# Applying the error's rows in half passes: key tiles 0 and 1 of a test-time-memory attention kernel

## The chip, the cores and the metric

One Trainium2 chip, one core. The metric is device time in microseconds (us) of one launch, lower is better.

## What is computed

Two layers over 8 sequences of 512 tokens with 128 features, all in fp32. Each layer is `x = x + s * g`, with `s` from a sequence mixer and `g` a SiLU of a feed-forward part. The change lies in the second layer's mixer, a memory that is trained while it reads. Per head (8 of them) and chunk of 64 tokens, the gradient of a two-matrix MLP's loss is taken, run through momentum and decay, added to the weights, and read with the queries:

```python
grads = jax.vmap(jax.grad(chunk_loss), ...)(mem_ws, flat(keys), lr, flat(values))
surprise = -grads
momentum = _assoc_scan(gm, surprise)
updates = _assoc_scan(gd, momentum)
w0 = mem_w0 + updates[0]
w1 = mem_w1 + updates[1]
x = jnp.einsum('bhncd,bhnde->bhnce', q, w0)
vals = jnp.einsum('bhncd,bhnde->bhnce', jax.nn.silu(x), w1)
```

The feed-forward part of that layer sends each token to one of 8 experts.

## The kernel before

The kernel never forms the updated weights. The update of a weight matrix is a weighted sum over earlier tokens of key times error, so reading it with a query is a score (key by query) times a coefficient, applied to the error's rows. This is linear attention with per-chunk coefficients, once for each of the two matrices.

After the first layer, `attend` runs 64 heads (8 batches by 8 heads). Its `step(f, s, z)` is written once for each engine, and every engine runs its own instructions strictly in that order. One step holds the front of head n + 1 (f), the second half of head n (s) and the end of head n - 1 (z). In batches 2 to 6 (`X_FIRST` to `X_LAST`) a step also carries one block x of 128 tokens of an expert's feed-forward: 40 steps in all. I call them expert heads, the others plain heads.

In a step TensorE (`pe`) does the following.
- It projects head f to U, EB and QA, and computes the second scores of head s, `scores(..., p_s1)`. In an expert head it transposes the block's rows (L813).
- It computes the product with s_2 into EB (the prediction's error) and the product of xs_2 into VB. To VB it adds `apply(VB, err_t, v_p1, k)`, with four key tiles i of 450, 322, 194 and 66 query columns.
- It does the expert block's first product (L828, expert heads), transposes err (L834) and multiplies err back through w1 into U (err_high, w4t).
- It computes the first scores of head f, transposes du, projects with w_x, and runs `apply(XB, du_t, v_p0, n)`. Then come the expert block's second product, the output product (L864) and the sums of squares (L868).

A product is either plain fp32, which the profile shows as two records, or `product(...)`: both operands are split into a high and a low fp32r half, and three passes high*high, high*low, low*high are added. The split costs a copy to fp32r (ScalarE) and a subtract (VectorE or GpSimd, called POOL in the profile). Before the change, both applies are plain fp32.

The scores get their coefficients on VectorE (`dve`): `weigh` multiplies the four tiles in the order 0, 1, 3, 2 (`SC_ORDER`) into p_sb and counts v_p1 (or v_p0) up after tiles 0, 3 and 2:

```python
                        if i != 1:
                            last.then_inc(done, 1)
```

In an expert head weigh comes after xf, the block's scaled input, which waits for the transpose L813. After weigh VectorE makes q_sb (L1109, L1111; the first of these counts v_q, and TensorE may overwrite U only after it), err_low (L1115), and du (L1118) after TensorE's product.

ScalarE (`act`) copies results out of PSUM and makes high halves: xs, s, th, qa, err, vals, sq, err_t, hid (expert heads), du_t, sq_mid. In heads 1 to 8 `scale_rows` (four rows) and in batch 7 `gate_rows` (four rows of a finished batch) stand ahead of du_t.

POOL makes the low halves of s, qa and sq, the root rs (which waits for VectorE's ms) and rg, which VectorE's sum of the outputs waits for before it weighs. In heads 6 to 13 it also issues four scatters each, in heads 5 to 10 it makes `starts`. In batch 7 it multiplies a finished batch by its gate (L1251), and VectorE adds the residual (L1164) before the next ms.

## Time and profile before

| | |
|---|---|
| median of 3 runs | 1116.36 us |
| the runs | 1113.86, 1116.40, 1116.36 us |
| the profiled execution's own time | 1116.89 us |
| its span on the core (first to last instruction) | 1115.1 us |
| mean granted TensorE clock | 0.988 of full speed |

The profile is of one execution. PE is TensorE's matmuls and PEld its weight loads, DVE is VectorE, ACT ScalarE, POOL GpSimd. Matmuls overlap in a pipeline and their ends are modelled, so two that follow each other closely show durations that add up to more than the time they take together. A row gives a group's first start, its length, the engine, the line of the kernel, the operation with output and inputs by name, the shapes and the count. Behind some stands the idle time before it and what ended that.

### The profile page before, as it was taken

Reading aid. Unit: us, or ns where it says so; the run is one execution under the profiler, and the core shown is the slowest. Engines: PE = TensorE matmul, PEld = TensorE weight load, DVE = VectorE, ACT = ScalarE, POOL = GpSimd, SP = SyncE. Lnnn points to the kernel's source line nnn. Section 1 sums busy time; section 2 is a strip of 40 time slices with the busy share of each in tenths; the row PEclk is TensorE's granted clock in tenths of the full one; section 3 lists DMA queues with packets and bytes.
Section 4 is the critical chain, followed back from the end, with each engine's and each line's share of the span. In section 5 each row is a group of like instructions: output and inputs, shape, how many; then the busy total and the mean of one; then the engine's idle time right before and its main releaser. Section 6 shows DMA issues by size and latency. Waiting matters only on the chain. (4 is left out here: it accounts for less than half of the span.)

```text
span 1115.1 us, 19052 instructions
## 1 busy us (share of the span) xinstructions
PE 1073.0 (96%) x6613; PEld 900.3 (81%) x6613; DVE 678.8 (61%) x1752; ACT 677.0 (61%) x1356; POOL 561.4 (50%) x574
## 2 busy tenths in 40 slices
PE   6999799999999999999999999999999999999994
PEld 4666588888888888888888888888888888888783
DVE  5887566766765555565555555565556555566664
ACT  5776366666655656565556655565656555566663
POOL 6885244478874444344534444344434454444453
PEclk9999699999999999999999999999999999999998
DMA  7210300000030000000000000000000000011221
GB/s 204 81 44 29 104 1 1 1 15 30 20 96 14 19 10 9 8 21 10 9 11 9 19 11 8 9 20 11 8 8 11 20 10 6 3 53 49 69 69 42
DMA packets 42129, 32.66 MB, mean 29 GB/s; under 512 B 4042, under 2 KB 36652, under 8 KB 41900
## 3 DMA queue, kind: packets, MB, share of 16 engines
q1 hardware_dynamic: 38484, 25.93, 8.1%
q0 software_dynamic: 2304, 4.74, 1.3%
q8 instruction: 54, 0.88, 0.3%
q10 hardware_dynamic: 1248, 0.79, 0.2%
q14 instruction: 39, 0.32, 0.1%
HBM read 18.30 MB, written 13.41 MB: 28 GB/s over the span
## 5 line engine op out<-in xcount | busy, mean ns | idle before, releaser
L1040 DVE TENSOR_TENSOR p_sb<-bank,coef 128x512 f32<-128x512 f32 (+3 forms) x512 | 218.7, 483 | 3.1 <-PE bank L749 2.6
L1232 POOL TENSOR_TENSOR sq_rest<-sq,sq_high 128x450 f32<-128x450 f32 x64 | 67.0, 1048 | 243.7 <-ACT sq_high L934 243.7
L772 PE MATMUL bank<-p_sb,du_t 128*128 128x450 f32 (+3 forms) x512 | 130.1, 397 | 4.4 <-ACT du_t L950 4.4
L772 PE MATMUL bank<-p_sb,err_t 128*128 128x450 f32 (+3 forms) x512 | 132.9, 402 | 0.2 <-DVE p_sb L1040 0.2
L772 PEld LDWEIGHTS bank<-p_sb,du_t 128*128 128x128 f32 x512 | 82.1, 190 | 48.9 <-issue 23.9
L772 PEld LDWEIGHTS bank<-p_sb,err_t 128*128 128x128 f32 x512 | 83.7, 190 | 45.6 <-DVE p_sb L1040 25.2
L1236 POOL TENSOR_TENSOR sq_low<-sq_rest,sq_mid 128x450 bf16<-128x450 f32 x64 | 67.5, 1054 | 104.3 <-ACT sq_mid L953 104.1
L1093 DVE SCALAR_TENSOR_TENSOR acc<-bank,rg,acc 128x128 f32<-128x128 f32 x224 | 62.8, 343 | 68.0 <-POOL rg L1220 68.0
L903 ACT ACTIVATE xs<-bank 128x450 f32<-128x450 f32 x64 | 35.0, 547 | 107.4 <-PE bank L772 107.4
L1118 DVE SCALAR_TENSOR_TENSOR du<-q_sb,bank 128x512 f32<-128x512 f32 x64 | 44.1, 689 | 89.0 <-PE bank L749 89.0
L1216 POOL TENSOR_TENSOR rs<-ms,neg_half 128x4 f32<-128x4 f32 x64 | 80.5, 1258 | 28.2 <-DVE ms L1075 26.8
L1207 POOL TENSOR_TENSOR s_low<-s_sb,s_high 128x512 fp32r<-128x512 f32 x64 | 82.6, 1291 | 21.6 <-ACT s_high L911 21.4
L909 ACT ACTIVATE s_sb<-bank 128x512 f32<-128x512 f32 x64 | 38.3, 598 | 88.5 <-PE bank L749 88.4
L930 ACT COPY vals<-bank 128x450 f32<-128x450 f32 x64 | 34.3, 536 | 88.8 <-PE bank L772 88.8
L1246 POOL DMA_INDIRECT ffn_rows<-xl_all,ids x40 | 41.5, 1038 | 83.9 <-DVE xl_all L1126 83.9
L1126 DVE TENSOR_TENSOR xl_all<-bank,xl_all 128x128 f32<-128x128 f32 x40 | 11.7, 292 | 117.2 <-PE bank L858 117.2
L1207 POOL TENSOR_TENSOR qa_low<-qa,qa_high 128x450 fp32r<-128x450 f32 x64 | 74.4, 1163 | 13.6 <-ACT qa_high L921 13.3
L924 ACT COPY err<-bank 128x512 f32<-128x512 f32 x64 | 37.6, 587 | 60.1 <-PE bank L749 60.1
L864 PE MATMUL bank<-w_out,vals 128*128 128x128 f32 (+1 forms) x512 | 67.4, 274 | 0.6 <-ACT vals L930 0.6
L864 PEld LDWEIGHTS bank<-w_out,vals 128*128 128x128 f32 (+1 forms) x512 | 60.0, 179 | 0.9 <-ACT vals L930 0.9
L950 ACT COPY du_t<-bank 128x512 f32<-128x512 f32 x64 | 37.3, 582 | 26.7 <-PE bank L848 26.7
L764 PE MATMUL bank<-qa,yb 128*128 128x66 f32 (+1 forms) x256 | 52.9, 288 | 0.0
(297 smaller groups left out, 3094.5 us busy)
## 6 DMA issues: line engine op xcount, KB each, us to landing
sorted_rows<-coef SPq DMA_DIRECT2D x5, 516.0 KB, 5.0
rows<-sorted_rows SPq DMA_DIRECT2D x40, 64.5 KB, 1.8
x<-in_L_attn_inputs SPq DMA_DIRECT2D x8, 256.0 KB, 5.5
x_rows<-x SPq DMA_DIRECT2D x8, 256.0 KB, 2.3
ew<-in_L_ffn_w SPq DMA_DIRECT2D x8, 256.0 KB, 4.0
attn_out<-acc SPq DMA_DIRECT2D x7, 256.0 KB, 2.1
ew<-attn_out SPq DMA_DIRECT2D x7, 256.0 KB
ew<-ffn_rows SPq DMA_DIRECT2D x8, 192.0 KB
```

The lines of the kernel that those rows point to most:

```text
L764: last = pe.matmul(out, left[:, (i - 2) * P:(i - 1) * P], right[:, P * i:], start=True, stop=True)
L772: last = pe.matmul(out[:, P * i:QW], rows[:, i, :], p_sb[:, P_COL[i]:P_COL[i] + QW - P * i], start=False, stop=True, skip_group_check=True)
L864: pe.matmul(VB[0:r, t * P:t * P + P], vals[:, t * P:t * P + r], m.w_out[:, s[1], :], start=True, stop=True)
L909: nc.scalar.activation(s_sb[h % 2][:], U[:], ACT.Silu).then_inc(a_s, 1)
L1040: last = nc.vector.tensor_tensor(dst, src, w, ALU.mult)
L1093: last = nc.vector.scalar_tensor_tensor(sums, o, g, sums, ALU.mult, ALU.add)
L1118: nc.vector.scalar_tensor_tensor(du[:], q_sb[:], 0.5, U[:], ALU.mult, ALU.mult).then_inc(v_du, 1)
L1207: nc.gpsimd.tensor_tensor(parts[1][:], whole[:], parts[0][:], ALU.subtract).then_inc(done, 1)
L1216: nc.gpsimd.tensor_tensor(rs[:], ms[:], m.neg_half[:, 0:T], ALU.pow).then_inc(g_rs, 1)
L1232: nc.gpsimd.tensor_tensor(sq_rest[:], sq[:], sq_3[0][:], ALU.subtract).then_inc(g_rest, 1)
L1236: nc.gpsimd.tensor_tensor(sq_3[2][:], sq_rest[:], sq_3[1][:], ALU.subtract).then_inc(g_lo, 1)
L1246: nc.gpsimd.indirect_dma_start(m.ffn_rows, bass.IndirectOffsetOnAxis(ids[r][:, 0:1], axis=0), y[r], None).then_inc(s_y[r], 16)
```

## The change

Only the apply of the error's rows changes its arithmetic; that of du stays plain fp32. Key tiles 0 and 1 of it become three passes of halves each. The rows err_t of tiles 0 and 1 are split in high and low (err_t2), as are the weighed scores of these tiles (p_2). Tiles 2 and 3 stay plain fp32 and are now applied first, in the order 3, 2, then 0, 1.

For that ScalarE gets two copies p_high behind qa_high, makes err_t in two copies of 256 columns (the first to th, which is free by then), and makes errt_high behind du_t. VectorE gets two subtracts p_low behind weigh, and q_sb moves behind err_low. POOL gets the subtract errt_low behind its last scatter, ahead of starts and of the next head's rs. ScalarE's scaled and gated rows are now done two by two, the first pair ahead of vals, the second behind sq_mid (`rows_of`). To make room in SBUF, du uses err's tile, sq_rest sq's, and token_q and per_token lie in m.amd. The semaphores' counts follow.

```diff
-        err_t = sb("err_t", [P, T, D])
-        du = sb("du", [P, S])
+        err_t, err_t2 = sb("err_t", [P, 2, D]), pair("errt2", [P, 2, D])
+        du = err
         du_t = sb("du_t", [P, T, D])
-        p_sb = sb("p_sb", [P, P_COLS])
+        p_sb, p_2 = sb("p_sb", [P, P_COLS]), pair("p2", [P, 2 * QW - P])
...
-        sq_rest = sb("sq_rest", [P, QW])
...
-        token_q = sb("token_q", [P, 3, NT])
+        token_q = m.amd[:, :, E + 3:].rearrange("p n a -> p a n")[:, 0:3, :]
...
-                def apply(out, rows, made, n):
-                    for i in SC_ORDER:
+                def apply_plain(out, rows, made, n, tiles=SC_ORDER):
+                    for i in tiles:
                         if i != 3:
                             pe.wait_ge(made, SC_BANKS * n + {0: 1, 1: 2, 2: 3}[i])
                         last = pe.matmul(out[:, P * i:QW], rows[:, i, :], p_sb[:, P_COL[i]:P_COL[i] + QW - P * i],
                                          start=False, stop=True, skip_group_check=True)
+                    return last
+
+                def apply(out, plain, halves, made, n, high, low):
+
+                    pe.wait_ge(made, SC_BANKS * n + 3)
+                    for i in (3, 2):
+                        pe.matmul(out[:, P * i:QW], plain[:, i - 2, :], p_sb[:, P_COL[i]:P_COL[i] + QW - P * i],
+                                  start=False, stop=True, skip_group_check=True)
+                    for i in (0, 1):
+                        cols = QW - P * i
+                        p_high, p_low = (part[:, QW * i:QW * i + cols] for part in p_2)
+                        pe.wait_ge(high, 2 * n + i + 1)
+                        for rows in halves:
+                            pe.matmul(out[:, P * i:QW], rows[:, i, :], p_high, start=False, stop=True, skip_group_check=True)
+                        pe.wait_ge(low, 2 * n + i + 1)
+                        last = pe.matmul(out[:, P * i:QW], halves[0][:, i, :], p_low, start=False, stop=True, skip_group_check=True)
                     return last
...
-                        pe.wait_ge(a_et, k + 1)
+                        pe.wait_ge(g_el, k + 1)
                         product(VB[:, 0:QW], [w[:] for w in w1], [part[:] for part in xs_2])
-                        apply(VB, err_t, v_p1, k).then_inc(p_v, 1)
+                        apply(VB, err_t, err_t2, v_p1, k, a_p1, v_l1).then_inc(p_v, 1)
...
-                        pe.wait_ge(a_et, n + 1)
+                        pe.wait_ge(a_et, 2 * n + 1)
                         project(XB, m.w_x, f, SHIFT)
                         pe.wait_ge(a_dt, n + 1)
-                        apply(XB, du_t, v_p0, n).then_inc(p_x, 1)
+                        apply_plain(XB, du_t, v_p0, n).then_inc(p_x, 1)
...
+                def p_high_of(made, n, i, done):
+
+                    cols = QW - P * i
+                    act.wait_ge(made, SC_BANKS * n + i + 1)
+                    nc.scalar.copy(p_2[0][:, QW * i:QW * i + cols], p_sb[:, P_COL[i]:P_COL[i] + cols]).then_inc(done, 1)
...
+                def rows_of(s, tiles):
+
+                    k, c = n_of(s), last_head(s)
+                    if c is not None and c > 0:
+                        gate_rows(c - 1, tiles)
+                    if 1 <= k <= B:
+                        scale_rows(k - 1, tiles)
...
+                        act.wait_ge(g_el, n)
...
+                        p_high_of(v_p1, k, 0, a_p1)
+                        p_high_of(v_p1, k, 1, a_p1)
+                    if f is not None:
                         act.wait_ge(p_e, n + 1)
                         act.wait_ge(p_d, n)
                         nc.scalar.copy(err[:], EB[:]).then_inc(a_err, 1)
                         act.wait_ge(a_err, n + 1)
                         nc.scalar.copy(err_2[0][:], err[:]).then_inc(a_eh, 1)
+                        rows_of(s, (0, 1))
...
-                    if f is not None:
-                        act.wait_ge(p_et, n + 1)
-                        nc.scalar.copy(err_t[:].rearrange("p t d -> p (t d)"), XB[:]).then_inc(a_et, 1)
                     if x is not None:
                         act.wait_ge(p_h, x + 1)
                         for k4 in range(FB):
                             last = nc.scalar.activation(hid[:, k4, :], QA[:, k4 * P:k4 * P + P], ACT.Relu, bias=w1s[:, PAR + 2 + k4:PAR + 3 + k4])
                         last.then_inc(a_h, 1)
-                    c = last_head(s)
-                    if c is not None and c > 0:
-                        gate_rows(c - 1)
-                    if s is not None and 1 <= k <= B:
-                        scale_rows(k - 1)
                     if f is not None:
+                        act.wait_ge(p_et, n + 1)
+                        act.wait_ge(v_g, n + 1)
+                        nc.scalar.copy(th[:, 0:2 * D], XB[:, 0:2 * D])
+                        nc.scalar.copy(err_t[:].rearrange("p t d -> p (t d)"), XB[:, 2 * D:]).then_inc(a_et, 1)
                         act.wait_ge(p_dt, n + 1)
                         nc.scalar.copy(du_t[:].rearrange("p t d -> p (t d)"), EB[:]).then_inc(a_dt, 1)
+                        act.wait_ge(a_et, 2 * n + 1)
+                        nc.scalar.copy(err_t2[0][:].rearrange("p t d -> p (t d)"), th[:, 0:2 * D]).then_inc(a_et, 1)
                     if s is not None:
                         act.wait_ge(g_rest, k + 1)
-                        nc.scalar.copy(sq_3[1][:], sq_rest[:]).then_inc(a_mid, 1)
+                        nc.scalar.copy(sq_3[1][:], sq[:]).then_inc(a_mid, 1)
+                    if s is not None:
+                        rows_of(s, (2, 3))
...
+                def p_low_of(made, n, i, done):
+
+                    cols = QW - P * i
+                    p = p_sb[:, P_COL[i]:P_COL[i] + cols]
+                    dve.wait_ge(made, 2 * n + i + 1)
+                    high, low = (part[:, QW * i:QW * i + cols] for part in p_2)
+                    nc.vector.tensor_tensor(low, p, high, ALU.subtract).then_inc(done, 1)
...
+                        p_low_of(a_p1, k, 0, v_l1)
+                        p_low_of(a_p1, k, 1, v_l1)
                     if f is not None:
+                        dve.wait_ge(a_eh, n + 1)
+                        nc.vector.tensor_tensor(err_2[1][:], err[:], err_2[0][:], ALU.subtract).then_inc(v_el, 1)
...
-                        dve.wait_ge(a_eh, n + 1)
-                        nc.vector.tensor_tensor(err_2[1][:], err[:], err_2[0][:], ALU.subtract).then_inc(v_el, 1)
...
+                        pool.wait_ge(a_et, 2 * n + 2)
+                        flat = [part[:].rearrange("p t d -> p (t d)") for part in err_t2]
+                        nc.gpsimd.tensor_tensor(flat[1], th[:, 0:2 * D], flat[0], ALU.subtract).then_inc(g_el, 1)
```

On TensorE, in an expert head, from the product of xs_2 to the block's first product. Before, with the semaphores that each row waits for:

```order
L749 MATMUL bank<-xs_high,w1n_high 128x450 [waits a_et,v_acc]
L749 MATMUL bank<-xs_low,w1n_high 128x450
L749 MATMUL bank<-xs_high,w1n_low 128x450
L772 MATMUL bank<-p_sb,err_t 128x450 [waits v_p1]
L772 MATMUL bank<-p_sb,err_t 128x322 [waits v_p1]
L772 MATMUL bank<-p_sb,err_t 128x66
L772 MATMUL bank<-p_sb,err_t 128x194 [waits v_p1]
L828 MATMUL bank<-xl_all 128x128 [waits a_qa,v_xf]
```

and now:

```order
L749 MATMUL bank<-xs_high,w1n_high 128x450 [waits g_el,v_acc]
L749 MATMUL bank<-xs_low,w1n_high 128x450
L749 MATMUL bank<-xs_high,w1n_low 128x450
L780 MATMUL bank<-p_sb,err_t 128x66 [waits v_p1]
L780 MATMUL bank<-p_sb,err_t 128x194
L787 MATMUL bank<-p_high,errt_high 128x450 [waits a_p1]
L787 MATMUL bank<-p_high,errt_low 128x450
L789 MATMUL bank<-p_low,errt_high 128x450 [waits v_l1]
L787 MATMUL bank<-p_high,errt_high 128x322 [waits a_p1]
L787 MATMUL bank<-p_high,errt_low 128x322
L789 MATMUL bank<-p_low,errt_high 128x322 [waits v_l1]
L844 MATMUL bank<-xl_all 128x128 [waits a_qa,v_xf]
```

The wait for v_p1 was one per tile (tile 0's first) and is now one for all, ahead of tile 3; tiles 0 and 1 are six passes with waits for ScalarE (a_p1) and VectorE (v_l1).

On VectorE, in an expert head, from the block's scaled input (L1102, now L1147) on. Before:

```order
L1102 TENSOR_SCALAR xl_all<-bank,xl_all 128x128 [waits p_t,v_w]
L1040 TENSOR_TENSOR p_sb<-bank,coef 128x512 [waits p_s1,p_x]
L1040 TENSOR_TENSOR p_sb<-bank,coef 128x384 [waits p_s1]
L1040 TENSOR_TENSOR p_sb<-bank,coef 128x128
L1040 TENSOR_TENSOR p_sb<-bank,coef 128x256 [waits p_s1]
L1109 SCALAR_TENSOR_TENSOR q_sb<-bank,s_sb 128x512 [waits a_s,a_tu]
L1111 SCALAR_TENSOR_TENSOR q_sb<-thu,q_sb 128x512 [waits v_q]
L1115 TENSOR_TENSOR err_low<-err,err_high 128x512 [waits a_eh]
```

and now:

```order
L1147 TENSOR_SCALAR xl_all<-bank,xl_all 128x128 [waits p_t,v_w]
L1077 TENSOR_TENSOR p_sb<-bank,coef 128x512 [waits p_s1,p_x]
L1077 TENSOR_TENSOR p_sb<-bank,coef 128x384 [waits p_s1]
L1077 TENSOR_TENSOR p_sb<-bank,coef 128x128
L1077 TENSOR_TENSOR p_sb<-bank,coef 128x256 [waits p_s1]
L1087 TENSOR_TENSOR p_low<-p_sb,p_high 128x450 [waits a_p1]
L1087 TENSOR_TENSOR p_low<-p_sb,p_high 128x322 [waits a_p1]
L1155 TENSOR_TENSOR err_low<-err,err_high 128x512 [waits a_eh]
L1158 SCALAR_TENSOR_TENSOR q_sb<-bank,s_sb 128x512 [waits a_s,a_tu]
L1160 SCALAR_TENSOR_TENSOR q_sb<-thu,q_sb 128x512 [waits v_q]
```

Two subtracts are added, and err_low now stands ahead of both steps of q_sb.

On ScalarE, in an expert head, from the high half of qa on. Before:

```order
L921 CAST qa_high<-qa 128x450 [waits a_qa]
L924 COPY err<-bank 128x512 [waits p_d,p_e]
L926 CAST err_high<-err 128x512 [waits a_err]
L930 COPY vals<-bank 128x450 [waits p_o,p_v]
L932 ACTIVATE sq<-vals 128x450 [waits a_v]
L934 CAST sq_high<-sq 128x450 [waits a_sq]
L937 COPY err_t<-bank 128x512 [waits p_et]
L941 ACTIVATE xl_all<-bank,xl_all 128x128 [waits p_hh]
```

and now:

```order
L952 CAST qa_high<-qa 128x450 [waits a_qa]
L899 CAST p_high<-p_sb 128x450 [waits v_p1]
L899 CAST p_high<-p_sb 128x322 [waits v_p1]
L959 COPY err<-bank 128x512 [waits p_d,p_e]
L961 CAST err_high<-err 128x512 [waits a_err]
L966 COPY vals<-bank 128x450 [waits p_o,p_v]
L968 ACTIVATE sq<-vals 128x450 [waits a_v]
L970 CAST sq_high<-sq 128x450 [waits a_sq]
L974 ACTIVATE xl_all<-bank,xl_all 128x128 [waits p_hh]
L974 ACTIVATE xl_all<-bank,xl_all 128x128 x3
L979 COPY thu<-bank 128x256 [waits v_g,p_et]
L980 COPY err_t<-bank 128x256
```

Two copies stand ahead of err; the copy err_t is halved and moved behind the block's hidden layer (L941, now L974), and errt_high stands ahead of sq_mid.

## Rows read from the trace of the kernel before

**Rows 1.** The page's part 1: busy time of each engine, share of the span, instructions

```profile
PE 1073.0 (96%) x6613; PEld 900.3 (81%) x6613; DVE 678.8 (61%) x1752; ACT 677.0 (61%) x1356; POOL 561.4 (50%) x574
```

**Rows 2.** Windows view, batch 7: length, busy us (count) PE, PEld, DVE, ACT, POOL, clock, DMA

```profile
1010.00:1090.00 80.00, 77.12 (x468) 64.65 (x468) 52.52 (x133) 53.37 (x106) 39.34 (x38) 1.00 0.20 61
```

**Rows 3.** Timeline, TensorE, an expert head: start us, length us, engine, line, operation

```profile
712.33 0.31 PE L749 MATMUL bank<-xs_high,s_high 128*128 128x322 f32 x1
712.48 0.31 PE L749 MATMUL bank<-xs_low,s_high 128*128 128x322 f32 x1
...
714.14 0.37 PE L749 MATMUL bank<-xs_high,w1n_high 128*128 128x450 f32 x1
714.35 0.37 PE L749 MATMUL bank<-xs_low,w1n_high 128*128 128x450 f32 x1
...
714.77 2.12 PE L772 MATMUL bank<-p_sb,err_t 128*128 128x450 f32 x8
716.73 1.05 PE L828 MATMUL bank<-xl_all 128*128 128x128 f32 x8
...
717.97 0.48 PE L749 MATMUL bank<-err_high,w4t_high 128*128 128x512 f32 x1
```

**Rows 4.** Timeline, TensorE, a plain head: apply, its tiles 3 and 2, what follows

```profile
300.44 2.01 PE L772 MATMUL bank<-p_sb,err_t 128*128 128x450 f32 x8
...
301.74 0.55 PE L772 MATMUL bank<-p_sb,err_t 128*128 128x66 f32 x3
...
302.29 0.27 PE L834 MATMUL bank<-ident,err 128*128 128x128 f32 x1
...
302.64 0.48 PE L749 MATMUL bank<-err_high,w4t_high 128*128 128x512 f32 x1
```

**Rows 5.** Timeline, VectorE's weigh in that expert head; TensorE and VectorE, the last one

```profile
714.04 1.68 DVE L1040 TENSOR_TENSOR p_sb<-bank,coef 128x512 f32<-128x512 f32 x4
...
982.82 0.65 PE L772 MATMUL bank<-p_sb,err_t 128*128 128x450 f32 x1
...
983.34 0.42 DVE L1040 TENSOR_TENSOR p_sb<-bank,coef 128x256 f32<-128x256 f32 x1
```

**Rows 6.** Timeline, ScalarE, the expert head

```profile
714.34 0.59 ACT L924 COPY err<-bank 128x512 f32<-128x512 f32 x1 [0.95 <-PE bank L749]
714.96 0.62 ACT L926 CAST err_high<-err 128x512 fp32r<-128x512 f32 x1
```

**Rows 7.** Timeline, VectorE and ScalarE, the plain head (the first is tile 2's weighing)

```profile
300.07 0.41 DVE L1040 TENSOR_TENSOR p_sb<-bank,coef 128x256 f32<-128x256 f32 x1
...
300.40 0.68 DVE L1109 SCALAR_TENSOR_TENSOR q_sb<-bank,s_sb 128x512 f32<-128x512 f32 x1
301.11 0.85 DVE L1111 SCALAR_TENSOR_TENSOR q_sb<-thu,q_sb 128x512 f32<-128x512 f32 x1
...
300.65 0.62 ACT L926 CAST err_high<-err 128x512 fp32r<-128x512 f32 x1
```

**Rows 8.** The page's part 5, applies of du; timeline, a head of batch 7

```profile
L772 PE MATMUL bank<-p_sb,du_t 128*128 128x450 f32 (+3 forms) x512 | 130.1, 397 | 4.4 <-ACT du_t L950 4.4
...
1045.47 1.65 ACT L883 ACTIVATE ew<-ew,token_q 128x128 f32<-128x128 f32 x4
...
1046.69 0.37 PE L749 MATMUL bank<-y_high,w_x_low 128*128 128x450 f32 x1
1047.64 0.65 PE L772 MATMUL bank<-p_sb,du_t 128*128 128x450 f32 x1 [0.57 <-ACT du_t L950]
```

**Rows 9.** Timeline, POOL in head 8, and TensorE's product that follows

```profile
253.52 0.79 POOL L1203 TENSOR_TENSOR ew<-lr_gate,starts 128x256 f32<-128x256 f32 x1
254.27 1.44 POOL L1216 TENSOR_TENSOR rs<-ms,neg_half 128x4 f32<-128x4 f32 x1
...
256.04 1.29 POOL L1207 TENSOR_TENSOR s_low<-s_sb,s_high 128x512 fp32r<-128x512 f32 x1
...
257.38 0.50 PE L749 MATMUL bank<-s_high,w1n_high 128*128 128x512 f32 x1
```

More of the change, by code:

```diff
@@ L698, in attend @@
         a_s, a_th, a_qa, a_err, a_et, a_xs, a_v, a_sq, a_dt = (sem(f"a_{k}") for k in ("s", "tu", "qa", "err", "et", "xs", "v", "sq", "dt"))
-        a_sh, a_qh, a_eh, a_xh, a_hi, a_mid = (sem(f"a_{k}") for k in ("sh", "qh", "eh", "xh", "hi", "mid"))
+        a_sh, a_qh, a_eh, a_xh, a_hi, a_mid, a_p1 = (sem(f"a_{k}") for k in ("sh", "qh", "eh", "xh", "hi", "mid", "p1"))
         v_q, v_g, v_du, v_p0, v_p1, v_ms, v_acc, v_y, v_xl, v_el = (
             sem(f"v_{k}") for k in ("q", "g", "du", "p0", "p1", "ms", "acc", "yb", "xl", "el"))
+        v_l1, g_el = sem("v_l1"), sem("g_el")
         g_rs, g_rg, g_sl, g_ql, g_rest, g_lo = (sem(f"g_{k}") for k in ("rs", "rg", "sl", "ql", "rest", "lo"))
@@ L787, in routing @@
                         rows = FREE[:, 0:3 * NT].rearrange("p (a n) -> p a n", a=3)
-                        pe.matmul(rows, m.ahead, m.per_token[:], start=True, stop=False)
+                        pe.matmul(rows, m.ahead, m.per_token, start=True, stop=False)
                         pe.matmul(rows[:, :, 0:NT - 1], m.behind, m.per_token[:, :, 1:], start=False, stop=True).then_inc(p_shift, 1)
@@ L878, in _, with gate_rows @@
             def _(act):
-                def gate_rows(c):
+                def p_high_of(made, n, i, done):
+                    cols = QW - P * i
+                    act.wait_ge(made, SC_BANKS * n + i + 1)
+                    nc.scalar.copy(p_2[0][:, QW * i:QW * i + cols], p_sb[:, P_COL[i]:P_COL[i] + cols]).then_inc(done, 1)
+                def gate_rows(c, tiles):
                     act.wait_ge(v_f, c + 1)
-                    for t in range(T):
+                    for t in tiles:
                         n = c * T + t
@@ L884, in gate_rows, with scale_rows @@
                     last.then_inc(a_g, 1)
-                def scale_rows(c):
+                def scale_rows(c, tiles):
                     act.wait_ge(v_top, 1)
-                    for t in range(c * T, c * T + T):
+                    for t in (c * T + t for t in tiles):
                         last = nc.scalar.mul(m.xl_all[:, t, 0:D], m.xl_all[:, t, 0:D], m.rr[:, 2, t:t + 1])
@@ L961, in step @@
                     if f is None and s is None:
-                        gate_rows(B - 1)
+                        gate_rows(B - 1, (0, 1))
+                        gate_rows(B - 1, (2, 3))
                 nc.scalar.copy(w1[0][:], m.w1n[:]).then_inc(a_made, 1)
@@ L1167, in finish_batch @@
                     q = (B - 1) % 2
-                    dve.wait_ge(a_g, B)
+                    dve.wait_ge(a_g, 2 * B)
                     dve.wait_ge(v_acc, B * H)
@@ L1235, in step @@
                         pool.wait_ge(g_rest, k + 1)
-                        nc.gpsimd.tensor_tensor(sq_3[2][:], sq_rest[:], sq_3[1][:], ALU.subtract).then_inc(g_lo, 1)
+                        nc.gpsimd.tensor_tensor(sq_3[2][:], sq[:], sq_3[1][:], ALU.subtract).then_inc(g_lo, 1)
                         scatter(s, 3)
+                    if f is not None:
+                        pool.wait_ge(a_et, 2 * n + 2)
+                        flat = [part[:].rearrange("p t d -> p (t d)") for part in err_t2]
+                        nc.gpsimd.tensor_tensor(flat[1], th[:, 0:2 * D], flat[0], ALU.subtract).then_inc(g_el, 1)
                     if s is not None and k == 0:
@@ L1366, in program @@
         m.place = sb("place", [P, NT], U32)
[L1367 removed]
+        m.per_token = m.amd[:, :, E:E + 3].rearrange("p n a -> p a n")
         m.blk_e = sb("blk_e", [P, NB], I32)
```

10 lines of the change are left out of this document (5 added, 5 removed).

## The prediction

> **What bounds the kernel now.** I read the page's busy shares first: TensorE is busy 96% of the span, its weight loads, which run beside it, 81%, every other engine near 60% or less [rows 1]. TensorE's granted clock is 1.00 in the last batch too, where it has its most frequent waits [rows 2]. Next I read TensorE in order of time in one head that also carries an expert block [rows 3] and in one that doesn't [rows 4]: each product starts where the one before has issued its columns. So TensorE's queue sets the end, and two questions decide the change: how much shorter that queue gets, and who is now late for it. The second is read from the other engines beside it [rows 5 to 9].
>
> Ends of matmuls are modelled, so I measure a matmul by the distance of starts.
>
> **What TensorE saves.** A fp32 apply of tiles 0 and 1 (450 and 322 columns, two records each) takes 301.74 - 300.44 = 1.30 us [rows 4]. A half pass of 450 columns takes 714.35 - 714.14 = 0.21 us (0.205 unrounded) and one of 322 takes 712.48 - 712.33 = 0.15 [rows 3]. Three of each: 0.615 + 0.45 = 1.065. Saving: 0.235 us a head, 63 heads or so, 14.8 us. Tiles 3 and 2 stay fp32 at 302.29 - 301.74 = 0.55 [rows 4], so the new apply is 0.55 + 1.065 = 1.615 long against 1.85.
>
> **What the new order costs in the 40 expert heads.** Before, apply could begin when tile 0 was weighed. Now its first wait is for all three counts of v_p1, that is for the end of VectorE's whole weigh. In an expert head VectorE starts to weigh only after the block's input is scaled, and the weigh runs from 714.04 to 715.72 [rows 5]. TensorE has issued its last half product at 714.55 + 0.20 = 714.75 (it follows the one at 714.35 by another 0.205) [rows 3]. So VectorE is 0.97 late. A wake costs something too: tile 0's weighing ends at 714.72 (0.68 of the four), the first matmul starts at 714.77, and its group lasts 716.73 - 714.77 = 1.96 instead of the 1.85 of a head without a wait, so 0.05 + 0.11 = 0.16 from VectorE's end to full pace. Before: 1.96 + 0.02 = 1.98 from 714.75 to the group's end. After: 0.97 + 0.16 + 1.615 = 2.74. That is **+0.76 us**. The head that ends the stretch shows the same distance: TensorE starts at 982.82, the weigh ends at 983.34 + 0.42 = 983.76, 0.94 later [rows 5] (0.95 in the head above). TensorE's later work moves as a block, since VectorE's weigh hangs on TensorE's transpose of the block's rows, which sits ahead of the wait, so nothing is caught up: 40 x 0.76 = **30.4 us**.
>
> Are the halves then in time? ScalarE's copy for tile 0 can start at 714.78 and the one for tile 1 at 715.44, when tile 3 is weighed; their lengths have no row, between the 0.57 to 0.62 of full copies and zero; I take 0.57 and 0.46 by columns, so 715.9 at the latest. VectorE's two subtracts then end by 716.75 (0.63 and 0.5, from its 512-column rate [rows 7]), and TensorE wants them at 716.8 and 717.3. They fit. ScalarE's err copy moves from 714.34 to 715.8, its high half from 714.96 to 716.4 to 717.05 [rows 6]; VectorE's err_low and, now behind it, q_sb are done at 718.4. TensorE wants q_sb before the product at 717.97 [rows 3], now 718.73. Cover left: about 0.2 us. It is the thinnest one here.
>
> **The 15 heads of batches 0 and 1 without a block.** Here VectorE weighs early: at 300.07 + 0.41 = 300.48 it is through, 0.04 behind TensorE [rows 4, 7]. But the move of q_sb behind the subtracts and err_low now bites, with no block's product as cover. ScalarE: copy for tile 1 from 300.2 to 300.65, err from 300.6, its high half 301.2 to 301.8, against 300.65 before [rows 7]. VectorE: err_low from 301.87 to 302.55, q_sb 0.07 before its end, as at 300.40 against 300.48 [rows 7], done 303.16, TensorE at pace 0.16 later, 303.3. It began that product at 302.64, at pace 302.72 [rows 4]. So +0.6; the other heads have 0.34 to 0.63 by where their weigh ends, in all **+7.0 us**. Before, some of these heads lost time to du_t, queued on ScalarE behind the four scaled rows; two rows now go where ScalarE is idle, two after du_t: the applies of du stood idle for du_t 4.4 us in all, 6 x 0.57 of that in batch 7, which leaves 1.0; a wait costs 0.27 more than its idle time shows (under batch 7), in four or five heads, so I take back **2.3 us** [rows 8].
>
> **POOL.** It gets the 256-column errt_low ahead of rs, and ScalarE's errt_high copy sits ahead of sq_mid, which releases sq_low. By columns from 1.29 for 512 [rows 9] the one costs 0.65, the other some 0.3. In five heads POOL also issues four scatters and makes the starts, and has no slack: starts ends 253.52 + 0.79 = 254.31, rs begins at 254.27, and TensorE starts its product 0.05 after s_low ends (256.04 + 1.29 = 257.33, then 257.38) [rows 9]. So 0.85 in each of five heads, 0.5 in all in the three with scatters alone: **+4.8 us**. In expert heads POOL waits for VectorE's block result at that place, and nothing is added.
>
> **Batch 7.** Four gate rows (1.65 us) hold du_t back, and TensorE begins the apply of du 0.84 late: 1046.69 + 0.20 = 1046.89, then 1047.64 and 0.10 of wake [rows 8]. The idle time shown there is 0.57, so 0.27 more is hidden in modelled ends. That wait goes, six times. But POOL's product of the finished batch, VectorE's sum and then ms and rs follow sq_low in line, 0.95 later as above, and q_sb costs 0.4. Net +0.5 a head: **+3.2**, the seventh head +0.4. Tail: apply of the last head waits for the whole weigh, +0.75, and sq_mid no longer waits for gate rows, -0.3: **+0.5**, both taken from the same steps.
>
> SBUF sharing (du in err, the copies in th) adds waits, but on events long past; no DMA is added. Cost nothing.
>
> **Sum.** 30.4 + 7.0 - 2.3 + 4.8 + 3.2 + 0.4 + 0.5 = +44. The 14.8 saved are inside these terms. The profiled execution took 1116.9 us (span 1115.1), 0.5 over the median: 1160.9 there, **1160 us** against the median of 1116.4.
>
> **Rules weighed.** VectorE's step with two SBUF inputs took 0.85 at 301.11, the one before it, of the same 512 columns but with one input from PSUM, 0.68 [rows 7]; the change adds two more of the first kind. I leave them at full pace: in plain heads 1.4 us lie between the end of the weigh and err_low, enough for both. The Trainium skill, "GPSIMD Engine Reference", section 1, says that POOL and VectorE share their SBUF interfaces and contend when a VectorE instruction has two SBUF inputs. The trace agrees with that, by 0.17. Applied to err_low too, in all 23 heads without a block, it would add 3.9 us to the sum.
>
> **Rivals.**
> *A, faster.* TensorE reaches the new wait when the weigh is over, and all passes saved count: 1116.4 - 14.8 - 7.3 of du_t waits = 1094, not slower than before. It decides at the place between the last half product and tile 3: it needs the weigh to end by 714.75 rather than 715.72. Rows 5 speak against it, in every expert head. Chance 0.03; a result within 0.3% needs a mixture and has 0.02.
> *B, only the expert heads pay.* ScalarE and POOL find the room elsewhere: 1116.4 + 30.4 - 1 = 1146. For it: VectorE and ScalarE are idle for 39% [rows 1]. Chance 0.08.
> *C, the thin cover goes.* Copies or subtracts take 0.5 longer together than taken: q_sb stalls expert heads by 0.3, +12: 1172. Chance 0.07.
> *D, the clock.* Pauses of 1 us in 16 bring TensorE's clock down. Priced by rows: at the lower level, each of 40 pauses followed by 1 us at half pace gives +20: 1180. Against it, the granted clock is 1.00 through batch 7 with its waits of 0.84 [rows 2, 8]. Chance 0.02. The Trainium skill, "TensorE: Matmul & The Clock Gate", section on HAM oscillation, warns that pauses between groups of matmuls can send the clock back to the lower level again and again. No row here shows it.
> *E, the forecast.* 0.78. Its own bounds: wake 0.05 to 0.25 a head (-4, +4), halves' copies (0 to +5), plain heads 0 to 9, POOL 0 to 8.
>
> **Numbers.** 1160, range 1146 to 1171: it takes in B and nearly C. Faster 0.03, within 0.3% (3.3 us, about what a measurement can tell) 0.02, slower 0.95.
>
> **What would show it.** In an expert head TensorE should stand idle about 0.9 us between the last half product and the 66-column product of p_sb, released by VectorE, and the head should be 0.76 longer; the halves' products should be back to back at 0.2 and 0.15. In plain heads the wait should be ahead of err_high's product, released by q_sb; du_t waits should be gone. No pause ahead of tile 3 would make the forecast wrong at its root; a second pause in expert heads, ahead of err_high, would be C.

## The result, and the profile after

The changed kernel takes **1169.1 us** (median of 4 runs, 1166.04 to 1170.09) against 1116.24 before: 1.048 times as long, 95% interval 1.046 to 1.050. The forecast was 1160, range 1146 to 1171. The profiled execution took 1168.4 us, its span is 1166.7, 51.6 more than before.

The page's part 1, of the kernel after (busy us of each engine, share of the span, instructions), which answers to [rows 1]:

```profile
PE 1075.2 (92%) x6741; PEld 915.2 (78%) x6741; DVE 755.0 (65%) x1880; ACT 760.8 (65%) x1612; POOL 608.2 (52%) x638
```

TensorE's busy time is nearly what it was, but in a longer span: 96% became 92%. So the time went into waits. Which ones, the view of waits of the same kernel tells (engine, what waits, who released it: us in total, times, longest):

```profile
PE bank L780 <- DVE p_sb L1077: 35.2, 41, 0.9
PE bank L749 <- DVE q_sb L1158: 9.7, 24, 1.5
PE bank L749 <- POOL s_low L1254: 7.7, 14, 0.9
...
PE bank L789 <- DVE p_low L1087: 1.6, 7, 0.6
```

There are 41 waits of 0.86 for VectorE's weigh (the 40 expert heads and the last head), 24 for q_sb (one in each plain head), and 14 for POOL. The wait for du_t of [rows 8] is gone; that apply now stands with no idle time in the page's part 5:

```profile
L772 PE MATMUL bank<-p_sb,du_t 128*128 128x450 f32 (+3 forms) x512 | 128.7, 394 | 0.0
```

The expert head of [rows 3, 5, 6] lies at 749 us now. Its timeline (start, length, engine, line, operation; in brackets the idle time before):

```profile
748.26 1.68 DVE L1077 TENSOR_TENSOR p_sb<-bank,coef 128x512 f32<-128x512 f32 x4
...
748.98 1.12 ACT L899 CAST p_high<-p_sb 128x450 fp32r<-128x450 f32 x2 [1.38 <-DVE p_sb L1077]
749.86 1.02 DVE L1087 TENSOR_TENSOR p_low<-p_sb,p_high 128x450 fp32r<-128x450 f32 x2
750.00 0.82 PE L780 MATMUL bank<-p_sb,err_t 128*128 128x66 f32 x4 [0.86 <-DVE p_sb L1077]
...
751.55 0.30 PE L789 MATMUL bank<-p_low,errt_high 128*128 128x322 f32 x1
751.70 1.05 PE L844 MATMUL bank<-xl_all 128*128 128x128 f32 x8
751.89 0.68 DVE L1158 SCALAR_TENSOR_TENSOR q_sb<-bank,s_sb 128x512 f32<-128x512 f32 x1
...
752.94 0.48 PE L749 MATMUL bank<-err_high,w4t_high 128*128 128x512 f32 x1
```

The weigh ends at 749.94, TensorE starts 0.06 later after 0.86 of idle time, the group is through at 751.70 (1.70 with the wake; forecast 0.11 + 1.615), and q_sb is ready at 752.57, 0.37 ahead of the product that wants it.

To see where the 51.6 us lie I measured, in both traces, the distance between the starts of four matmuls of TensorE that each head has once. These marks are the third passes of err's and xs's products and the first of s's and y's. The differences, after minus before, in us:

| stretch | part | forecast | measured |
|---|---|---|---|
| 40 expert heads | between xs's product and err's | +30.4 | +29.2 |
| heads 0 to 15 | between xs's product and err's | +7.0 | **+11.2** |
| heads 0 to 15 | du_t | -2.3 | -2.4 |
| heads 0 to 15 | s_low | +4.8 | **+7.2** |
| batch 7, its seven steps | all | +3.6 | +3.9 |
| after them | | +0.5 | +0.7 |
| first layer, up to head 0's product of err | | 0 | +1.1 |
| rest of heads 0 to 15 | | 0 | +0.8 |

Of the last row, 0.47 stands in one place: four small matmuls of head 5 that read `per_token`. TensorE in that head, before and then after:

```profile
219.17 0.35 PE L788 MATMUL bank<-per_token,ew 128*128 128x96 f32 x2
219.36 0.27 PE L789 MATMUL bank<-per_token,ew 128*128 128x93 f32 x1
...
223.20 0.64 PE L804 MATMUL bank<-amd,ew 128*128 128x96 f32 x2
223.65 0.42 PE L805 MATMUL bank<-amd,ew 128*128 128x93 f32 x1
```

From the pair to the next one it takes 0.19 before and 0.45 after, with no wait between. The change had put this tile into m.amd, where the elements that a pass reads one after the other lie 24 apart instead of side by side. Every kernel below that has the tile there shows the same 0.5 in head 5, also the last one, which makes no half passes in these heads; none shows it where the tile lies as before. No run moved the tile alone.

TensorE's clock has no part in this. The windows view of the kernel after (columns as in [rows 2]), for the expert heads and batch 7:

```profile
400.00:1030.00 630.00, 596.51 (x3972) 527.03 (x3970) 383.00 (x966) 405.00 (x880) 294.73 (x308) 1.00 0.04 10
1060.00:1140.00 80.00, 75.54 (x457) 62.37 (x457) 60.33 (x137) 58.66 (x124) 40.62 (x41) 1.00 0.20 61
```

Two terms are larger than forecast. The plain head that answers to [rows 4, 7] shows the first, in the same view:

```profile
298.04 1.16 POOL L1254 TENSOR_TENSOR qa_low<-qa,qa_high 128x450 fp32r<-128x450 f32 x1
...
298.24 1.87 DVE L1087 TENSOR_TENSOR p_low<-p_sb,p_high 128x450 fp32r<-128x450 f32 x2
...
299.75 0.47 PE L789 MATMUL bank<-p_low,errt_high 128*128 128x450 f32 x1 [0.16 <-DVE p_low L1087]
300.03 0.68 DVE L1155 TENSOR_TENSOR err_low<-err,err_high 128x512 fp32r<-128x512 f32 x1
...
300.63 0.68 DVE L1158 SCALAR_TENSOR_TENSOR q_sb<-bank,s_sb 128x512 f32<-128x512 f32 x1
...
301.45 0.47 PE L749 MATMUL bank<-err_high,w4t_high 128*128 128x512 f32 x1 [0.33 <-DVE q_sb L1158]
```

The pair p_low takes 1.87, in the expert head 1.02. The tile's view gives the first of the pair alone, here and in the expert head (minimum, median and maximum of one instruction, in ns):

```profile
L1087 DVE TENSOR_TENSOR p_low<-p_sb,p_high x1: 1462/1462/1462, 298.2 to 298.2; 128x450 fp32r<-128x450 f32 x1
...
L1087 DVE TENSOR_TENSOR p_low<-p_sb,p_high x1: 620/620/620, 749.9 to 749.9; 128x450 fp32r<-128x450 f32 x1
```

POOL's qa_low runs beside the slow one for 0.96 us and beside the other not at all. Heads 7 to 13 all show 1.45 to 1.53, and head 6, where 1.16 overlap, 1.96. The kernel before had shown the same effect on q_sb's second step, which has two inputs in SBUF as well. It takes 0.69 alone, and in head 7 of before, with 0.75 us of POOL's qa_low beside it:

```profile
230.79 1.31 DVE L1111 SCALAR_TENSOR_TENSOR q_sb<-thu,q_sb 128x512 f32<-128x512 f32 x1
```

The second is POOL's queue in the step that answers to [rows 9], with VectorE's xs_low in it:

```profile
258.01 1.47 POOL L1283 TENSOR_TENSOR sq_low<-sq,sq_mid 128x450 bf16<-128x450 f32 x1 [0.79 <-ACT sq_mid L987]
...
260.65 0.74 POOL L1288 TENSOR_TENSOR errt_low<-thu,errt_high 128x256 fp32r<-128x256 f32 x1
261.34 1.26 POOL L1250 TENSOR_TENSOR ew<-lr_gate,starts 128x256 f32<-128x256 f32 x1
262.57 1.04 POOL L1263 TENSOR_TENSOR rs<-ms,neg_half 128x4 f32<-128x4 f32 x1
...
261.09 0.85 DVE L1126 TENSOR_TENSOR xs_low<-xs,xs_high 128x450 fp32r<-128x450 f32 x1
```

errt_low took 0.74 where I had 0.65. The product `starts` took 0.79 before, when it began ahead of xs_low; now it begins 0.25 behind xs_low and takes 1.26. rs, pushed behind both, takes 1.04 instead of 1.44. Starts and rs together thus cost nearly the same as before. The rest of the 1.14 us a head in heads 8 to 11 stands ahead of errt_low: sq_low takes 1.47 where it took 1.28 in the same head of before, and it waits for sq_mid.

### The profile page after: what moved, and what is told of

Its sections match the earlier page's. It is cut to its first block and busy times, and to the rows that moved or that the text cites. A ratio compares the mean times of both kernels' runs of the same rounds, so it can differ in the third digit from the quotient of the medians.

```text
span 1166.7 us, 19885 instructions
## 1 busy us (share of the span) xinstructions
PE 1075.2 (92%) x6741; PEld 915.2 (78%) x6741; DVE 755.0 (65%) x1880; ACT 760.8 (65%) x1612; POOL 608.2 (52%) x638
## 5 line engine op out<-in xcount | busy, mean ns | idle before, releaser
L1279 POOL TENSOR_TENSOR sq<-sq,sq_high 128x450 f32<-128x450 f32 x64 | 67.2, 1050 | 277.3 <-ACT sq_high L970 277.3
L1283 POOL TENSOR_TENSOR sq_low<-sq,sq_mid 128x450 bf16<-128x450 f32 x64 | 69.1, 1079 | 128.9 <-ACT sq_mid L987 128.9
L899 ACT CAST p_high<-p_sb 128x450 fp32r<-128x450 f32 (+1 forms) x128 | 65.8, 514 | 84.5 <-DVE p_sb L1077 77.9
L780 PE MATMUL bank<-p_sb,err_t 128*128 128x66 f32 (+1 forms) x256 | 51.6, 324 | 35.2 <-DVE p_sb L1077 35.2
L780 PEld LDWEIGHTS bank<-p_sb,err_t 128*128 128x128 f32 x256 | 33.9, 190 | 55.6 <-DVE p_sb L1077 55.2
L1087 DVE TENSOR_TENSOR p_low<-p_sb,p_high 128x450 fp32r<-128x450 f32 (+1 forms) x128 | 73.5, 616 | 0.0
L1165 DVE SCALAR_TENSOR_TENSOR err<-q_sb,bank 128x512 f32<-128x512 f32 x64 | 44.0, 688 | 38.8 <-PE bank L749 38.8
L1155 DVE TENSOR_TENSOR err_low<-err,err_high 128x512 fp32r<-128x512 f32 x64 | 44.2, 691 | 24.4 <-ACT err_high L961 24.3
```

Source lines behind the costliest of these rows:

```text
L780: pe.matmul(out[:, P * i:QW], plain[:, i - 2, :], p_sb[:, P_COL[i]:P_COL[i] + QW - P * i], start=False, stop=True, skip_group_check=True)
L899: nc.scalar.copy(p_2[0][:, QW * i:QW * i + cols], p_sb[:, P_COL[i]:P_COL[i] + cols]).then_inc(done, 1)
L1087: nc.vector.tensor_tensor(low, p, high, ALU.subtract).then_inc(done, 1)
L1155: nc.vector.tensor_tensor(err_2[1][:], err[:], err_2[0][:], ALU.subtract).then_inc(v_el, 1)
L1279: nc.gpsimd.tensor_tensor(sq[:], sq[:], sq_3[0][:], ALU.subtract).then_inc(g_rest, 1)
L1283: nc.gpsimd.tensor_tensor(sq_3[2][:], sq[:], sq_3[1][:], ALU.subtract).then_inc(g_lo, 1)
```

## The experiments

Twelve kernels ran. "After" is the changed kernel, "before" the one before. Heads 0 to 15, the expert heads and batch 7 are compared by the marks above.

### The wait alone

Before, with one wait for all counts and the order 3, 2, 0, 1, still plain fp32:

```diff
-                        apply(VB, err_t, v_p1, k).then_inc(p_v, 1)
+                        apply(VB, err_t, v_p1, k, (3, 2, 0, 1)).then_inc(p_v, 1)
```

(with the tuple given, `apply` waits once, for `SC_BANKS * n + 3`).

> The kernel before, all arithmetic unchanged, with two edits to the apply of the error's rows: one wait for all three counts of v_p1 ahead of it, and the tile order 3, 2, 0, 1. No copy, no subtract, no half pass. Theory (the wait for VectorE's whole weigh is the main cost): in each of the 40 expert heads TensorE starts 0.97 + 0.16 after its last half product instead of 0.13 after it, so +1.0 us a head, 40 in all, 1 over the 15 plain heads, 1 in the tail: 1158. Rival (the extra work on ScalarE, VectorE and POOL is what costs, and the wait is hidden): 1116. The change itself, with the same wait, measured 1169.

Measured: 1157.5 us, ratio 1.035 [1.033, 1.037]. Expert heads +39.4 us, 0.985 each. In heads 0 to 15 the stretch between xs's product and err's is 1.2 longer (a shorter start of head 0 hides that in their sum, +0.1), batch 7 is +0.2, and the stretch behind the last mark +1.0. That is what I expected, term by term. So in the expert heads the wait alone costs more than the whole change does. The difference of the two, 0.25 a head, is what the shorter passes give back.

### The block's product ahead of apply

After, with the `for k4 in range(FB)` loop of L844 moved ahead of `apply(VB, ...)`:

> The changed kernel with TensorE's first product of the expert block (four fp32 products, 0.89 us) moved ahead of the apply, into the pause. Theory: the pause ahead of tile 3 shrinks from 0.9 to 0.2 us, but the 0.66 gained ends at the next wait, VectorE's first step of q_sb, which in expert heads has a cover of only 0.26 us: net -0.26 a head, 1169 - 10 = 1159, and a new pause of 0.4 ahead of err_high's product released by q_sb. Rival (q_sb is not late in expert heads): -0.66 to -0.9 a head, 1134 to 1143.

Measured: 1159.0, ratio 1.037 [1.035, 1.039]. Expert heads -9.9, 0.25 each, and nothing in the other heads. The block's product fills the wait for the weigh, but it had been the cover of q_sb, and a new wait stands there. The view of waits of this kernel, and one head of it:

```profile
PE bank L749 <- DVE q_sb L1159: 26.0, 64, 1.5
```

```profile
745.81 0.60 PE L851 MATMUL bank<-ident,err 128*128 128x128 f32 x4
746.81 0.47 PE L749 MATMUL bank<-err_high,w4t_high 128*128 128x512 f32 x1 [0.40 <-DVE q_sb L1159]
```

All 64 heads wait for q_sb now. The cover in the expert heads was thus 0.25 thick by this run (forecast 0.2): what is gained before it is lost beyond that.

### q_sb's first step ahead of err_low

```diff
+                        nc.vector.scalar_tensor_tensor(q_sb[:], U[:], 1.0, s_sb[h % 2][:], ALU.add, ALU.subtract).then_inc(v_q, 1)
                         dve.wait_ge(a_eh, n + 1)
                         nc.vector.tensor_tensor(err_2[1][:], err[:], err_2[0][:], ALU.subtract).then_inc(v_el, 1)
-                        nc.vector.scalar_tensor_tensor(q_sb[:], U[:], 1.0, s_sb[h % 2][:], ALU.add, ALU.subtract).then_inc(v_q, 1)
```

> The changed kernel with VectorE's first step of q_sb ahead of err_low again (still behind the two subtracts). Theory: in the 22 plain heads TensorE waits for q_sb, 0.6 us behind err_low; with the swap it waits for err_low only, -0.44 a head; expert heads don't change: 1169 - 10 = 1159. Rival (plain heads are held by POOL, and q_sb's wait only stands in front of POOL's): 1169 within 2.

Measured: 1158.7, ratio 1.037 [1.035, 1.039]. Heads 0 to 15 -4.9, batch 7 -3.8, expert heads +0.9. The first layer, which this edit doesn't touch, was 2.6 us shorter in this trace than in that of the changed kernel, so the total flatters it: the edit is worth 8 to 9 us. What is left in the plain heads waits for err_low, 2.7 us in 9 heads.

### errt_low on VectorE

The subtract moves from POOL to VectorE, behind its second weigh:

> The changed kernel with errt_low (the low half of the error's rows, 256 columns) made by VectorE behind its weigh of head f instead of by POOL. Theory: POOL's 0.65 to 0.75 leaves the chain sq_low, errt_low, starts, rs, s_low in some seven heads of batch 0 and 1 and the chain sq_low, errt_low, gate product, sum, rs in six heads of batch 7: -0.7 x 13 = -9: 1160. Rival (the chain is held by the later sq_low alone): -2, 1167. Expert heads: no change under either.

Measured: 1162.1, ratio 1.039 [1.038, 1.041], 2 us short of what I expected. The wait for s_low lost 3.3 of its 7.2 us in heads 0 to 15, and 2.0 in batch 7. The view of waits of this kernel still has

```profile
PE bank L749 <- POOL s_low L1257: 3.2, 12, 0.4
```

so POOL's own subtract was about half of that term. The rest goes only in the last run of this section.

### VectorE's weigh ahead of the block's input

```diff
+                    if s is not None:
+                        dve.wait_ge(p_x, k + 1)
+                        weigh(s, p_s1, v_p1, k)
                     if x is not None:
...
                     if s is not None:
-                        dve.wait_ge(p_x, k + 1)
-                        weigh(s, p_s1, v_p1, k)
                         p_low_of(a_p1, k, 0, v_l1)
```

> The changed kernel with VectorE's weigh of head s ahead of the expert block's ids and xf in expert heads, so that it needn't wait for TensorE's transpose of the block's rows. Theory (the pause is VectorE's weigh queued behind xf): the weigh starts 1.2 us earlier and ends 0.2 ahead of TensorE's last half product, the pause is gone, and expert heads lose the 0.75 they paid and gain the saved passes and the old 0.13: -0.745 - 0.37 = -1.1 a head, 44.5 in all: 1125. Plain heads as in the changed kernel. Rival (the halves' copies and subtracts are then the next to be late): a new wait of 0.3 to 0.5 on p_low or q_sb in expert heads: 1137 to 1145.

Measured: 1125.2 (1124.85 to 1125.61), ratio 1.009 [1.007, 1.011]: 44 us for moving one call. All of it, 44.5 us, lies in the expert heads, 1.11 each. TensorE's timeline in such a head has the last half product of xs and the first tile back to back, with nothing idle:

```profile
724.10 0.36 PE L749 MATMUL bank<-xs_high,w1n_low 128*128 128x450 f32 x1
724.30 0.71 PE L780 MATMUL bank<-p_sb,err_t 128*128 128x66 f32 x4
724.72 0.51 PE L787 MATMUL bank<-p_high,errt_high 128*128 128x450 f32 x1
```

This is the condition of rival A, made true in the 40 expert heads alone. Nobody needs the block's input early: it used to be ready at the weigh's start, and TensorE takes it behind apply.

### The same move in the kernel before

> The kernel before with the same move of VectorE's weigh ahead of ids and xf, all arithmetic as before. Theory: only the 0.13 us that TensorE waited for tile 0 in the 40 expert heads goes: -5, 1111 to 1113. Rival (xf, now late, holds the block's first product): no change or slower, 1116 to 1120.

Measured: 1110.5 (1107.76 to 1112.86), ratio 0.996 [0.994, 0.997]. Expert heads -6.1, 0.15 each. The rows of before had 0.13 for it (1.98 instead of 1.85): with one wait a tile the late weigh cost no more than that. Between this run and the one above lies the change alone: -15.3 against -6.1 in the expert heads, so the half passes bring 9.2 us there, 0.23 each (0.235 by the rows of before).

### qa_low ahead of the first scatter

After, with POOL's order changed so that its subtract no longer stands beside p_low, but a scatter does:

```diff
-                        scatter(s, 0)
                         pool.wait_ge(a_qh, n + 1)
                         lacks(qa, qa_2, g_ql)
+                        scatter(s, 0)
```

> The changed kernel with POOL's subtract qa_low ahead of its first scatter in a step. In the changed kernel p_low of 450 columns took 0.62 us alone and 1.46 us in the eight heads with scatters, where qa_low ran beside it for 0.97. Theory (VectorE's step with two SBUF inputs all but stands still while POOL's subtract runs): qa_low is over before p_low starts, p_low takes 0.62 to 0.75 again, -0.4 in each of eight heads: -3.5, 1165.5. Rival (it is the scatter, a DMA issue, that slows it): the scatter now runs beside p_low, which stays at 1.4: no change.

Measured: 1166.6, ratio 1.046 [1.044, 1.048]. Heads 0 to 15 -3.5, all between xs's product and err's. The same place as above, POOL and VectorE in this kernel:

```profile
295.07 1.16 POOL L1254 TENSOR_TENSOR qa_low<-qa,qa_high 128x450 fp32r<-128x450 f32 x1
296.40 2.11 POOL L1246 DMA_INDIRECT sorted_rows<-xl_all,place  x1 [0.16 <-issue]
...
296.56 1.02 DVE L1087 TENSOR_TENSOR p_low<-p_sb,p_high 128x450 fp32r<-128x450 f32 x2
```

p_low's pair is back at 1.02 although POOL is busy beside it all the time, with a scatter. qa_low takes 1.16 in either place. So what slowed p_low is POOL's subtract, and of the two only VectorE's became slower.

### Four edits together

After, with the weigh first, q_sb's first step first, errt_low on VectorE, qa_low ahead of the scatter:

> The changed kernel with four moves at once: VectorE's weigh ahead of xf, first step of q_sb ahead of err_low, errt_low on VectorE, qa_low ahead of the first scatter. Sum of the single effects: 1169 - 44.5 - 8 - 5 - 3 = 1108, faster than the kernel before. If the expert heads have a new wait (rival of the run on weigh alone), 1120 to 1128.

Measured: **1100.8** (1100.43 to 1101.28), ratio 0.987 [0.985, 0.989]: faster than both kernels. Against before: expert heads -15.3, batch 7 -1.8, heads 0 to 15 +0.8. So where there is no block the change with its four moves brings next to nothing, although its split rows alone are worth more there, as the next run shows.

### The split rows alone

Before, with `rows_of` in its two parts and nothing else:

> The kernel before with the other part of the change alone: ScalarE's scaled and gated rows two by two, the first pair ahead of vals, the second behind sq_mid; all arithmetic as before. Theory: the waits for du_t go, 2.4 us in batches 0 and 1 and 5.1 in batch 7, of which heads 4 and 5 give 0.9 back at a wait for POOL's s_low (in the changed kernel that wait appeared there just as the wait for du_t went): -6.5, about 1109. Rival (each freed wait is taken up by POOL's chain sq_low, gate product, sum, rs): 1115 to 1116.

Measured: 1108.1 (1106.44 to 1110.28), ratio 0.993 [0.991, 0.994]. Heads 0 to 15 -1.7, batch 7 -4.2, and the sixth of batch 7's waits, 0.8, lies behind the last mark. du_t's waits give 2.4 and 4.2 us back, to the tenth what they gave in the changed kernel; 0.8 of the 2.4 is lost again in front of s_low, in heads 4 and 5.

### The split rows and the weigh first, no half passes

> The kernel before with the rows two by two and VectorE's weigh ahead of xf, still without any half pass in the applies. Theory: the two gains add up, -5.5 and -6.5: 1104. The four moves on the changed kernel measured 1100.8, so the half passes themselves, with all that they bring, would then be worth only 3 us of the 14.8 saved on paper. Rival (the moves share one slack): 1109.

Measured: 1104.0 (1100.75 to 1106.05), ratio 0.989 [0.987, 0.991]. Its interval overlaps that of the four edits, 0.985 to 0.989, so by time alone these two can't be told apart. The traces can: the half passes are 9.3 us ahead in the expert heads, and 2.4 behind in each of heads 0 to 15 and batch 7.

### A fifth edit that missed

The four, with ScalarE's errt_high behind sq_mid instead of ahead of it:

> The kernel with four moves, and as a fifth ScalarE's copy errt_high behind sq_mid instead of ahead of it. In its trace TensorE still waits 0.46 us for s_low in heads 7 to 11, and 0.4 in heads of batch 7, and sq_low starts after sq_mid, which stands 0.3 behind errt_high. Theory: -0.3 in each of some 12 heads: -3.5, 1097. Rival (errt_low on VectorE, now 0.5 later, holds VectorE's next work): no change or slower, 1101 to 1104.

Measured: 1105.7 (1103.59 to 1105.87), ratio 0.991 [0.989, 0.992]: not 1097, and slower than without. Heads 0 to 15 +0.8, batch 7 +1.8. VectorE and POOL in a step of batch 7 of this kernel:

```profile
1033.27 1.06 DVE L1175 TENSOR_TENSOR errt_low<-thu,errt_high 128x256 fp32r<-128x256 f32 x1 [0.64 <-ACT errt_high L988]
1034.26 2.14 DVE L1209 SCALAR_TENSOR_TENSOR ew<-ew,amd 128x128 f32<-128x128 f32 x4
1036.32 0.68 DVE L1216 TENSOR_TENSOR ew<-ew 128x512 f32<-128x512 f32 x1
1036.92 0.15 DVE L1120 TENSOR_SCALAR ms<-bank 128x3 f32<-128x3 f32 x1
...
1037.21 1.33 POOL L1268 TENSOR_TENSOR rs<-ms,neg_half 128x4 f32<-128x4 f32 x1 [1.75 <-DVE ms L1121]
```

errt_low waits 0.64 for its high half and takes 1.06 beside POOL's sq_low; behind it in VectorE's queue stand the finished batch's sums, then ms, and POOL's rs waits 1.75 for ms. With the four edits errt_low waited 0.17, and took 0.43. With a later high half I had made VectorE's queue longer than I made POOL's shorter, and the same s_low waits at the end of both.

### Half passes only in the expert heads

The four edits, but the 24 plain heads apply all tiles in plain fp32, with one wait a tile, and make no halves:

```diff
+        in_halves = lambda n: (X_FIRST * H <= n < (X_LAST + 1) * H)
...
+                        if in_halves(k):
+                            last = apply(VB, err_t, err_t2, v_p1, k, a_p1, v_l1)
+                        else:
+                            last = apply_plain(VB, err_t, v_p1, k, err_first[:])
...
-                    if s is not None:
+                    if s is not None and in_halves(k):
                         p_low_of(a_p1, k, 0, v_l1)
```

> The version of e8 (weigh first, q_sb's first step ahead of err_low, errt_low on VectorE, qa_low ahead of the first scatter), but with half passes only in the 40 expert heads; the other 24 apply the error's rows in plain fp32, in the order 0, 1, 3, 2 with one wait a tile, and make neither halves of rows nor of scores. Theory (half passes pay 0.23 us where TensorE stands between other products, and cost more than they bring where VectorE's and POOL's queues bind): expert heads as in e8, 15.3 below before; heads 0 to 15 as in e10, 1.5 below; batch 7 as in e10, 4.2 below. Together 21 below before, 1095 to 1096, and about 5 below e8. Rival (e8 and e10 are equal, the half passes bring nothing over the whole program, and what the trace shows in the expert heads is noise): 1101 to 1104. Further rival (the boundary heads, where the two kinds meet, or the additional tile cost something): over 1104.

Measured: **1094.1** (1092.29 to 1095.36, 5 runs), ratio 0.980 [0.978, 0.982], the fastest of all. Expert heads -15.5, batch 7 -4.2, heads 0 to 15 -1.9, where the theory had -15.3, -4.2 and -1.5. Its page's part 1, and what is left of the wait for s_low:

```profile
PE 1054.9 (97%) x6693; PEld 912.1 (83%) x6693; DVE 734.6 (67%) x1872; ACT 731.8 (67%) x1540; POOL 561.2 (51%) x574
```

```profile
PE bank L753 <- POOL s_low L1275: 0.8, 2, 0.4
```

## Why the prediction was right, and where it wasn't

The mechanism that makes up 30 of the 44 us was right, and an experiment shows it alone. The total was 9 us short, 2 inside the end of the range. By the marks the terms were 7.6 short; two of them, in heads 0 to 15, make 6.6 of that. Of the large terms only the expert heads' was too high, by 1.2, so little of the hit is errors that cancel.

**What bounds the kernel.** Right. TensorE's queue sets the end: the gains and losses of the twelve runs stand in it, as waits or as longer or shorter passes.

**The passes.** 0.235 us saved a head, measured 0.23 (between the fifth run and the sixth) and 0.25 (between the first and the changed kernel).

**Expert heads.** 0.76 forecast, 0.73 measured; the first run puts all of the loss on the new wait and the fifth takes it away. The thin cover of q_sb was 0.25, not 0.2, and held: rival C's wait (for q_sb) appeared in no expert head until the second run used the cover up.

**du_t.** -2.3 forecast, -2.4 measured, and the ninth run shows the same alone. I missed that two heads give 0.8 of it back at a wait for s_low, which the table counts there.

**Plain heads: mis-sized.** +7.0 forecast, +11.2 measured, in sixteen heads where I had counted fifteen (the one more has 0.3). The step that failed is "I leave them at full pace: in plain heads 1.4 us lie between the end of the weigh and err_low, enough for both". The pair p_low took 1.87 in the eight heads with scatters, and err_low, ready to go at 299.62 when err_high ended, started at 300.03. Moving POOL's subtract away took 3.5 us off; 7.7 is left, near the 7.0. I had looked for POOL's work beside VectorE's in the head of [rows 7] alone, where it had cost 0.17, and not asked what of POOL's would stand beside the *new* instructions. The Trainium skill, "GPSIMD Engine Reference", section 1, says that the two share their SBUF interfaces and contend when VectorE's instruction has two SBUF inputs. The trace agrees, and has the size, the overlap less 0.13: my 0.17 came from an overlap of 0.29, head 7 of before had already lost 0.62 to one of 0.75, and p_low lost 0.84 to one of 0.96. I had costed the rule on err_low, which stayed at 0.68; it bit on p_low.

**POOL: mis-sized.** +4.8 forecast, +7.2 measured. Of the step "by columns from 1.29 for 512 the one costs 0.65, the other some 0.3" the subtract itself took 0.74; taking it off POOL gave only 3.3 of the 7.2 back. Leaving out all halves in these heads gave the rest but 0.8, the part that the split rows cost by themselves. How that rest divides between errt_high ahead of sq_mid, sq_low's 1.47 and the scatters was not settled: the run that moved errt_high moved VectorE's subtract with it.

**Batch 7 and the tail.** +4.1 forecast, +4.6 measured. Here q_sb cost 0.6 in five of the seven heads and 0.35 in two, instead of 0.4, and POOL's later chain took just what du_t's gave back, instead of 0.1 more.

**First layer.** +1.1, which no term of mine covers. The first 0.5 lie ahead of head 0's product of s, where the twelve kernels of the experiments lie between -2.1 and +1.9 of before: that is no sign of the change. The other 0.6 is the change, in head 0, whose product of err waited 1.1 for err_low before and waits 1.5 for q_sb now.

**Sharing of SBUF.** "Cost nothing" was wrong by 0.5 us: no wait was added, but four matmuls of head 5 that read the moved tile became slower.

**The rivals.** A gave 1094 if TensorE never met the wait. In the changed kernel it always did; the fifth run made its condition true, and the expert heads then took its saving in full. B fell with plain heads at +11.2 and POOL at +7.2. C and D did not happen: no q_sb wait in expert heads, and a granted clock of 1.00 over 40 pauses of 0.86 us. The half pace that D was priced with stands in no row of before, so its 20 us were never tested.

## What to carry to other kernels

When a change cuts an engine's passes and adds a wait, look at who makes the last thing that the wait is for, and what stands ahead of it in that queue: here 1.1 us a head came from the order of two pieces on VectorE, and 0.23 from the passes. Apply such a change only where the helpers have room: the half passes, with all that they bring, gained 9 us in 40 heads and lost 5 in the other 24. And for every instruction added to VectorE or POOL, ask which of the other's will run beside it once it is there.

## What the runs showed of the hardware

A subtract on VectorE with two inputs in SBUF all but stands still while POOL subtracts: 1.46 us instead of 0.62, with 0.96 us of overlap. POOL's 1.16 is the same with and without it. The loss follows the overlap: the traces of the fourteen kernels together have 139 places where qa_low had begun before p_low or q_sb's second step and ran on beside it for over 0.15 us, and in each of them VectorE's instruction lost the overlap less 0.12 to 0.14 (0.24 of 0.38 in head 0 of the changed kernel).

With POOL's `starts` and VectorE's xs_low it was the one that began later that lost. In the changed kernel `starts` began 0.25 behind xs_low and took 1.26 instead of 0.79, with 0.59 of overlap. With the four edits it began 0.28 ahead, kept its 0.80, and xs_low took 1.02 instead of 0.61, with 0.53 of overlap. qa_low doesn't follow this: in six places p_low had begun first, and it lost 1.06 to 1.35 all the same, to an overlap of 1.16 (so in head 6 of the changed kernel), while qa_low kept its 1.16. Why the two differ is open.

A scatter's issue on POOL beside p_low doesn't slow it (0.62 again), but that issue took 2.11 there, and 1.06 in its old place. Whether VectorE's work is what lengthened it was not tested.

Four plain fp32 matmul passes of 93 to 96 columns with 128 rows took 0.47 us more when they read one input at every 24th element instead of side by side. No run moved that tile alone.
